# The causal triangle of the second pass added on TensorE, and the row minimum taken as one plain reduction over three key blocks

## The reference, cut to what matters

```python
# layer 0: x = x + self_attn(layer_norm(x), mask); x = x + ctx @ Wg.T + bg; x = x + mlp(layer_norm(x))
# layer 1:
def mha(x_q, x_kv, wq, wk, wv, wo, causal):
    q = (x_q @ wq).reshape(B, Sq, H, Dh) * (1.0 / np.sqrt(Dh))
    k, v = (x_kv @ wk).reshape(...), (x_kv @ wv).reshape(...)
    scores = jnp.einsum('bqhf,bkhf->bhqk', q, k)
    if causal:
        scores = jnp.where(jnp.tril(jnp.ones((Sq, Sk), dtype=bool)), scores, NEG_INF)
    p = jax.nn.softmax(scores, axis=-1)
    return jnp.einsum('bhqk,bkhf->bqhf', p, v).reshape(B, Sq, D) @ wo
x = layer_norm(targets); x = mha(x, x, sa_*, causal=True) + targets
y = mha(layer_norm(x), encoded, ca_*, causal=False) + x
out = y + relu(layer_norm(y) @ w1 + b1) @ w2 + b2
```

## Time and profile before

| | |
|---|---|
| median of 3 runs | 1569.3 us (1567.14 to 1570.04) |
| profiled execution | 1565.11 us, of that 1563.3 us span |
| mean granted TensorE clock | 0.986 of full |
| PE, DVE, ACT, POOL busy | 91%, 76%, 66%, 54% |
| pass 1 scores | from 609 us to 991 us |
| one mixed step of pass 1 | 22.47 us |

### The profile page before, as it was taken

How to read it: one execution, slowest core, us unless ns; L and a number is a source line. 1 busy time by engine, 2 the same in 40 slices (tenths; PEclk the granted TensorE clock), 3 DMA queues, 4 the chain that set the end, 5 groups by cost and what they waited for, 6 DMA issues and landing times.

```text
span 1563.3 us, 39199 instructions
## 1 busy us (share of the span) xinstructions
PE 1422.4 (91%) x13504; PEld 1168.1 (75%) x13504; DVE 1184.2 (76%) x3890; ACT 1024.5 (66%) x2073; POOL 839.2 (54%) x1144
## 2 busy tenths in 40 slices
PE   3889999999999999998888888889999999999986
PEld 3678888888888888876666666567777777777666
DVE  3998888888888888778877877877777676777642
ACT  4777777677777775566666666676566666656652
POOL 4455554545555565655555555555555565555534
PEclk8999999999999999999999999999999999999989
DMA  5554433334433444535546545644434334433300
GB/s 161 153 149 125 121 109 109 109 111 127 116 109 109 117 121 117 149 110 146 160 138 174 141 138 149 161 145 120 117 96 115 95 103 126 113 114 96 88 14 14
DMA packets 161587, 187.07 MB, mean 120 GB/s; under 512 B 15984, under 2 KB 136176, under 8 KB 161392
## 3 DMA queue, kind: packets, MB, share of 16 engines
q1 hardware_dynamic: 161392, 184.57, 41.2%
HBM read 125.78 MB, written 58.72 MB: 118 GB/s over the span
## 4 chain that ended last, share of the span: by engine, by line
PE 59%; DVE 15%; ACT 12%; issue 9%; POOL 3%; SPq 1%; DMA 1%; DVEq 0%; ACTq 0%; POOLq 0%
PE d_ps L485 25%; PE d_ps L751 8%; PE o_ps L622 7%; PE t_ps L558 6%; PE s_ps L544 6%; DVE prob L949 4%; PE t_ps L592 3%; ACT prob_t L801 3%; ACT q_stack L809 3%; PE m_ps L492 2%; DVE stats L955 2%; ACT h_f L887 2%; DVE top L934 1%; ACT tf_b L816 1%; DVE o_q L1030 1%
## 5 line engine op out<-in xcount | busy, mean ns | idle before, releaser
L801 ACT ACTIVATE prob_t<-t_ps 128x384 f32<-128x384 f32 (+1 forms) x512 | 277.2, 549 | 291.6 <-PE t_ps L592 185.4
L544 PE MATMUL s_ps<-k_stack,q_stack 96*128 96x256 bf16 (+1 forms) x1536 | 285.2, 267 | 45.5 <-DVE top L949 22.3
L792 ACT ACTIVATE prob<-prob,neg_max 128x256 f32<-128x256 f32 x512 | 232.7, 508 | 115.2 <-DVE neg_max L949 113.5
L1177 POOL TENSOR_TENSOR h_lo<-h_f,h_hi 128x512 fp32r<-128x512 f32 x128 | 164.7, 1287 | 119.1 <-DVE h_hi L1070 119.1
L544 PEld LDWEIGHTS s_ps<-k_stack,q_stack 96*128 96x128 bf16 x1536 | 114.9, 98 | 138.7 <-issue 45.6
L592 PE MATMUL t_ps<-q_stack,k_stack 108*128 108x256 bf16 (+1 forms) x1024 | 201.6, 263 | 16.5 <-ACT prob_t L801 13.6
L949 DVE CUSTOM_DVE_ANT_0 prob<-s_ps,bias_sb 128x256 f32<-128x256 f32 x512 | 193.0, 416 | 26.6 <-PE s_ps L544 24.5
L934 DVE TENSOR_REDUCE top<-s_ps 128x2 f32<-128x512 f32 x256 | 172.1, 681 | 48.2 <-PE s_ps L544 44.9
L949 DVE CUSTOM_DVE_ANT_0 prob<-s_ps,causal 128x128 f32<-128x128 f32 (+1 forms) x512 | 157.2, 351 | 46.2 <-PE s_ps L544 45.0
L622 PE MATMUL o_ps<-prob_t,v_sb 128*17 128x256 f32 (+1 forms) x3072 | 192.0, 368 | 0.0
L485 PE MATMUL d_ps<-x2t_hi,w_hi 128*128 128x256 f32 x512 | 157.0, 307 | 15.4 <-ACT k_f L874 10.5
(11 more groups left out here) (125 smaller groups left out, 3962.9 us busy)
## 6 DMA issues: line engine op xcount, KB each, us to landing
parts<-q_part SPq DMA_DIRECT2D x96, 192.0 KB, 2.3
parts<-k_part SPq DMA_DIRECT2D x96, 192.0 KB, 2.3
q_stack<-parts SPq DMA_DIRECT2D x96, 192.0 KB, 3.3
k_stack<-parts SPq DMA_DIRECT2D x96, 192.0 KB, 3.3
q_stack<-parts SPq DMA_DIRECT2D x96, 128.0 KB, 3.1
k_stack<-parts SPq DMA_DIRECT2D x96, 128.0 KB, 3.1
ct_kept<-ct_hl SPq DMA_DIRECT2D x16, 512.0 KB, 3.8
x_in<-x_mid SPq DMA_DIRECT2D x32, 256.0 KB, 3.3
```

Of the source, the lines that this page charges most:

```text
L544: last = mm(s_ps[:, h % 2, q * S:q * S + n], q_stack[0:ROWS, t.par, head_of(t, h), q * P:(q + 1) * P], k_stack[0:ROWS, t.par, head_of(t, h ...
L792: last = nc.scalar.activation(prob[:, h % 4, q, :], prob[:, h % 4, q, :], ACT.Exp, bias=neg_max[:, h % 4, q:q + 1], scale=-1.0)
L801: nc.scalar.activation(prob_t[:, h % 8, 0:n], t_ps[:, h % 2, 0:n], ACT.Exp, scale=-1.0)\
L1177: g.tensor_tensor(dst, a, b, ALU.subtract).then_inc(done, 1)
```

## The change

In pass 1 TensorE's query-major scores of a head are laid out as three neighbouring blocks of 128 keys: block 0 for query block 0, blocks 1 and 2 for query block 1. Behind each of the two score matmuls TensorE adds the triangle `later` to the diagonal block by a matmul with the identity, accumulating into the same bank. VectorE then takes one TENSOR_REDUCE over 128 x 3 x 128 for a head, which gives three minima. After the last head of a chunk it waits for its own reduction, folds the minima of blocks 1 and 2 into one with a small TENSOR_TENSOR and sets a new semaphore, `least`, for which GpSimd's split waits in place of `u_done`. The tile `causal` and its set-up on GpSimd go, as does the write to `prob` in pass 1.

```diff
@@ two_layers
-        top = sb("top", [P, 2, TT, CH])
+        top = sb("top", [P, 2, TT + 1, CH])
-        causal = sb("causal", [P, TT, S])
+        least = ev("least", CH, (1,))
@@ scores (TensorE)
+                if h == 0 and t.first and t.p == 1:
+                    pe.wait_ge(causal_made, 3)
                 for q in range(TT):
-                    n = (q + 1) * P if t.p == 1 else S
-                    last = mm(s_ps[:, h % 2, q * S:q * S + n], q_stack[0:ROWS, t.par, head_of(t, h), q * P:(q + 1) * P],
-                              k_stack[0:ROWS, t.par, head_of(t, h), 0:n], start=True, stop=True)
+                    at, n = (q * P, (q + 1) * P) if t.p == 1 else (q * S, S)
+                    last = mm(s_ps[:, h % 2, at:at + n], q_stack[0:ROWS, t.par, head_of(t, h), q * P:(q + 1) * P],
+                              k_stack[0:ROWS, t.par, head_of(t, h), 0:n], start=True, stop=t.p != 1)
+                    if t.p == 1:
+                        last = mm(s_ps[:, h % 2, 2 * q * P:2 * q * P + P], later[:, :], ident_bf[:, :],
+                                  start=False, stop=True)
                 last.then_inc(s_mm.sem, 1)
@@ score_guard (VectorE)
+                if t.p == 1:
+                    v.tensor_reduce(top[:, part, :, h % CH], s_ps[:, h % 2, 0:3 * P].rearrange("p (b k) -> p b k", k=P),
+                                    AX_X, ALU.min).then_inc(u_done.sem, 1)
+                    if h % CH == CH - 1:
+                        dve.wait_ge(u_done.sem, u_done.after(t, h + 1))
+                        v.tensor_tensor(top[:, part, 1, :], top[:, part, 1, :], top[:, part, 2, :], ALU.min)\
+                            .then_inc(least.sem, 1)
                     return
...
-                    bias = causal[:, q, 0:n] if t.p == 1 else bias_sb[:, t.par, q, 0:n]
-                    least = top[:, h // CH % 2, q, h % CH:h % CH + 1] if t.p == 1 else neg_max[:, h % 4, q:q + 1]
-                    last = v.tensor_tensor_reduce(prob[:, h % 4, q, 0:n], s_ps[:, h % 2, q * S:q * S + n], bias,
-                                                  1.0, HUGE, ALU.add, ALU.min, least)
@@ GpSimd
-            g.memset(causal[:, :, :], 0.0).then_inc(causal_made, 1)
-            g.affine_select(out=causal[:, :, :], in_=causal[:, :, :], compare_op=ALU.is_ge, fill=MASKED, base=0,
-                            pattern=[[P, TT], [-1, S]], channel_multiplier=1).then_inc(causal_made, 1)
@@ top_split
-                pool.wait_ge(u_done.sem, u_done.after(t, CH * (c + 1)))
+                if t.p == 1:
+                    pool.wait_ge(least.sem, least.after(t, c + 1))
+                else:
+                    pool.wait_ge(u_done.sem, u_done.after(t, CH * (c + 1)))
```

More of the change, by code:

```diff
@@ L579, in keyed_scores @@
                     pe.wait_ge(chosen, 8)
-                    pe.wait_ge(causal_made, 5)
+                    pe.wait_ge(causal_made, 3)
                 if h % CH == 0:
@@ L932, in score_guard @@
                 dve.wait_ge(s_mm.sem, s_mm.after(t, h + 1))
+                part = h // CH % 2
                 if t.p == 2:
-                    v.tensor_reduce(top[:, h // CH % 2, :, h % CH], s_ps[:, h % 2, :].rearrange("p (q k) -> p q k", q=TT),
+                    v.tensor_reduce(top[:, part, 0:TT, h % CH], s_ps[:, h % 2, :].rearrange("p (q k) -> p q k", q=TT),
                                     AX_X, ALU.min).then_inc(u_done.sem, 1)
+                    return
+                if t.p == 1:
[5 more added lines that the diff above has]
+                            .then_inc(least.sem, 1)
                     return
@@ L939, in score_guard @@
                     dve.wait_ge(t_mm.sem, t_mm.after(before, hb + 1))
-                if h == 0 and t.p == 0:
+                if h == 0:
                     dve.wait_ge(bias_done.sem, bias_done.after(t))
-                if h == 0 and t.first and t.p == 1:
-                    dve.wait_ge(causal_made, 3)
                 dve.sem_inc(passed, 1)
                 for q in range(TT):
-                    n = (q + 1) * P if t.p == 1 else S
-                    bias = causal[:, q, 0:n] if t.p == 1 else bias_sb[:, t.par, q, 0:n]
-                    least = top[:, h // CH % 2, q, h % CH:h % CH + 1] if t.p == 1 else neg_max[:, h % 4, q:q + 1]
-                    last = v.tensor_tensor_reduce(prob[:, h % 4, q, 0:n], s_ps[:, h % 2, q * S:q * S + n], bias,
-                                                  1.0, HUGE, ALU.add, ALU.min, least)
+                    last = v.tensor_tensor_reduce(prob[:, h % 4, q, :], s_ps[:, h % 2, q * S:(q + 1) * S],
+                                                  bias_sb[:, t.par, q, :], 1.0, HUGE, ALU.add, ALU.min,
+                                                  neg_max[:, h % 4, q:q + 1])
                 last.then_inc(u_done.sem, 1)
@@ L1160, in _ @@
             g.memset(minus_half[:, :], -0.5).then_inc(causal_made, 1)
-            g.memset(causal[:, :, :], 0.0).then_inc(causal_made, 1)
+            g.memset(later[:, :], 0.0).then_inc(causal_made, 1)
             pool.wait_ge(causal_made, 2)
-            g.affine_select(out=causal[:, :, :], in_=causal[:, :, :], compare_op=ALU.is_ge, fill=MASKED, base=0,
-                            pattern=[[P, TT], [-1, S]], channel_multiplier=1).then_inc(causal_made, 1)
-            g.memset(later[:, :], 0.0).then_inc(causal_made, 1)
-            pool.wait_ge(causal_made, 4)
             g.affine_select(out=later[:, :], in_=later[:, :], compare_op=ALU.is_ge, fill=MASKED, base=0,
@@ L1187, in top_split @@
                     pool.wait_ge(top_mm.sem, top_mm.after(before, cb + 1))
-                src, part = top[:, c % 2], top_part[:, c % 2]
+                src, part = top[:, c % 2, 0:TT], top_part[:, c % 2]
                 g.tensor_tensor(part[:, :, :, 0], src, zeros[:, :, :], ALU.add).then_inc(top_1.sem, 1)
@@ L1234, in slot @@
                         .then_inc(causal_made, 1)
-                    pool.wait_ge(causal_made, 6)
+                    pool.wait_ge(causal_made, 4)
                 if h == 10 and has(st.prev, (0,)):
```

## The result

The changed kernel takes 1570.94 us (median of 15 runs, 1568.2 to 1574.38), the kernel before in the same rounds 1564.87 us: ratio 1.0031 (of the means, 1570.9 and 1566.1 us), 95% interval 1.002 to 1.0041, so slower by 0.3%. The profiled execution took 1569.28 us, where that of before took 1565.11; the spans are 1567.1 and 1563.3 us.

What follows compares the result with a forecast made beforehand. Neither engine alone bounds the step; the chain alternates between TensorE and VectorE. +0.40 - 0.27 = +0.13 us a mixed step, +1.8 over 14, +1.2 for two tasks: 1568.1 profiled, 1572.3 us forecast; own range 1567 to 1578, overall 1558 to 1587.

Steps and rivals of the forecast that it cites:

- sign of being wrong on the slow side: A mixed step of pass 1 taking 23 us or more, where about 22.6 was forecast.
- A step made of two halves: Mixed step of 22.47 us: the chain holds TensorE for 10 us, then mainly VectorE for 12.4 us.
- TensorE's half: From 805.50 to o_q at 815.56, six heads' scores: the added triangles make it end 0.52 us later.
- the two covers: Waits in TensorE's half, for ScalarE's exponential and o_q, absorb 0.12 and 0.1 us of the added triangles.
- The handover: Between the halves: GpSimd's k_f moves 0.40 us, not 0.52, hiding 0.12; q_part's cast stays blocked and long.
- The port was not won: First rival, chance 0.13: q_part's cast wins the port shared with GpSimd, 0.98 us a step, about 1562 us.
- VectorE's minimum: Plain reduction of 384 a head: 547 ns to the result, 0.46 us start to start, saving 0.09 us.
- The fold: After each chunk's last minimum on VectorE: 0.12 us wait plus 0.07 for the instruction, 0.19 us a chunk.
- The far end of A: A is the step's VectorE half, 12.4 us: forecast -0.27 us, ends 0 and -0.45.
- the third rival: Chance 0.27: waits in TensorE's half hide nothing, VectorE saves nothing; +0.72 us a step, 1583 us.
- The two first tasks of pass 1: Beside the MLP of pass 0, chain mostly on TensorE: +1.2 us, at most +3.8, at least 0.
- VectorE as the bound of the whole step: Second rival, chance 0.10: VectorE bounds the step, -1.0 us each, -14 us over 14 steps, 1555 us.

Runs made afterwards that it cites:

- tri_only: The kernel before with TensorE's triangle added and VectorE left as it is: 1578.08 us, ratio to before 1.0081.
- tri_twice: The changed kernel with each triangle matmul issued twice: 1582.78 us, 1.0112 of before.
- fold_reduce: The changed kernel with the fold as a one-operand TENSOR_REDUCE, `top` moved to the end so no other tile moves: 1561.38 us, 0.9978 of before.
- old_places: The changed kernel with every tile but `top` back where the kernel before has it: 1577.47 us, 1.008 of before.
- shift32: The kernel before with 32 unused bytes a partition behind `top`: 1557.59 us, 0.9953 of before.
- all_at_64: The kernel before with 64 unused bytes ahead of the transposed activations and 96 behind `top`: 1557.03 us, 0.9956 of before.

## Why the prediction was right, and where it was not

The time came out at +0.3% where +0.2% was forecast, from a sum in which two errors met; that is luck. So is the closeness of 1570.94 to the forecast 1572.3 us: the latter starts from a median of three runs, 1569.3, that in the rounds of the result was 1564.87. The mixed step of 23.24 us is past the prediction's own sign of being wrong on the slow side, 23 us or more.

**A step made of two halves: right, TensorE's half a little too cheap.** TensorE's half, from the rows of minima at 807.42 to o_q at 818.10, is 10.68 us; it was 815.56 - 805.50 = 10.06. So +0.62 against +0.52 forecast. Of the two covers, ScalarE's exponential held: the third keyed scores start 2.88 us into the half (810.30) where it was 2.78, so 0.14 of the first two heads' 0.24 was absorbed. The wait for o_q hardly did: the rows of minima stand 4.99 us into the half where they stood at 4.68, so the next two heads lost 0.21 of their 0.24. The last two heads added their 0.24. And in the chain of waits the twelve matmuls of the projection behind the fifth head's scores take 1.49 us where they took 1.43, which the sum left out. That makes 0.62. tri_only's 0.65 for the whole step agrees, and tri_twice shows no cover for more.

**The handover: right.** The cast of q_part lasts 1.23 us (it was 1.35), and the next minimum starts 1.15 us after it where it was 1.28: -0.13 against -0.12 forecast. The port was not won, so that rival fell.
The Trainium skill's rule for the port that VectorE and GpSimd share (SBUF — State Buffer, SBUF: two separate sides), that the first holds it for its whole instruction, agrees: GpSimd's k_f starts at 818.26, 0.21 us ahead.

**VectorE's minimum: right in size.** The forecast of 547 ns to the result is what was measured; where a cast follows it, start to start, it is 0.47 us (806.51 - 806.04) against 0.46. The start of 0.04 us after TensorE's end is there too: 814.67 + 0.22 = 814.89, and the reduction starts at 814.93.

**The fold: the step that failed.** The prediction put it at 0.19 us a chunk, 0.12 for the wait and 0.07 for the instruction, and never set it beside GpSimd: it has the casts blocked, but for the fold even the far end, 0.35 us, is only the length of a reciprocal. Three folds cost about that. The fourth takes 0.87 us, beside GpSimd's subtraction of ot_lo. The half of VectorE from 819.62 to the next 830.66 (807.42 + 23.24) is 11.04 us where it was 805.50 + 22.47 - 817.21 = 10.76: +0.28, where -0.27 was forecast. Of this the blocked fold is 0.72 by fold_reduce; the remaining -0.44 is more than the -0.27 I gave. The far end of A is -0.45 in the prediction, but its own parts (-0.19 and -0.17) add up to -0.36 only. The cast of k_part was not blocked (0.41 us); what else gave more back is not shown. The step: +0.62 - 0.13 + 0.28 = +0.77 us, where I had +0.13. That is the price of the third rival, in which the covers fail, but mostly not by its mechanism: one cover held, A did save, and with the free fold the step is at +0.05.
I had read the page's rule on the port for casts and stopped there. The same passage of the Trainium skill (SBUF — State Buffer, SBUF: two separate sides) counts also a VectorE operation with two SBUF inputs against a GpSimd operation that reads SBUF, and that is the fold. By that rule the trace agrees: 0.87 us with two operands beside a subtraction that began first, 0.16 with one.

**The two first tasks of pass 1.** From mark 14 to 16 it is 67.61 us before and 69.06 now, +1.4, against +1.2 forecast; how it divides over their scores was not looked into.

**What I left out altogether: the tiles' places.** The diff's first line moves the tiles behind `top` by 32 bytes. It is worth 6 us in passes 0 and 2. The prediction took these passes as fixed and summed pass 1 alone. Without this gain the loss is 0.8% (old_places, 1577.47 us), four times the 0.2% forecast.

**VectorE as the bound of the whole step** fell: it still waits 1.15 us for the projection and 1.85 us for scores, and tri_only made the step longer. **The tensor_reduce rule** of the Trainium skill (VectorE: DVE Perf Modes, Rules for kernel authors), which calls it the slowest operation, is not borne out for these sizes: reductions of 256 and 128 elements take 413 and 282 ns, the custom minimum of the same sizes 418 and 284.

In sums for one mixed step: triangle +0.65 (tri_only), plain reductions -0.60 (fold_reduce against tri_only, 23.12 to 22.52), the blocked fold +0.72 (changed against fold_reduce). The price of the first triangle was measured beside the custom instruction alone. Even with the free fold the exchange is a small loss at equal places: fold_reduce takes 1561.38 us, shift32 1557.59. The two were timed in the same rounds, against the same runs of before.

## What to carry to other kernels

When the bound changes hands within a step, price an edit in the half where its engine holds the chain: 31 us of TensorE work and a lighter VectorE came to +0.05 us a step once nothing was blocked. Before adding even a tiny VectorE instruction with two SBUF operands, look at what GpSimd runs beside it; here a form with one operand took 0.16 us at the same place. And when a diff changes a tile's size, ask what stands behind it, and compare passes that the edit does not touch before explaining the total.

## What the runs showed of the hardware

- A move of the tiles behind `top`, matmul operands among them, by 32 bytes a partition changed the spacing of fp32r matmuls of 256 columns from 119 to 117 ns, and the kernel by 0.47% (shift32). A step of pass 0 took 36.54 us with no unused bytes, 36.29 with 32 and 36.57 with 96. That 64 bytes beyond a multiple of 128 is a fast place does not hold for all products (all_at_64). The cause within the memory or the engine is not settled.
- A VectorE TENSOR_TENSOR over 128 x 4 with both operands in SBUF that started 0.43 us into a GpSimd subtraction of 1.27 us took 0.87 us and ended with it, and 0.16 us where no such subtraction had more than 0.1 us to go; a TENSOR_REDUCE over 128 x 8 in its place took 0.16 beside the same subtraction.
- A plain reduction that waits for scores started 0.04 us after TensorE's last matmul, at one place before and one after; the custom instruction 0.19 us after it, at one place. The ends of matmuls are modelled.
